# Toeplitz tiles of a second causal convolution: loaded into 32 partitions and widened twice on chip, with taps copied eight channels at a time

## The chip, the cores and the metric

The kernel runs on one core of a Trainium2 chip. The metric is the device time of one execution in microseconds (us); lower is better. The work of the five engines (TensorE, VectorE, ScalarE, GpSimd and SyncE, which only issues transfers here) is written out by hand with semaphores; nothing is scheduled by a compiler.

## The reference, cut to what matters

The input u has 16 sequences of 512 positions and 256 channels. A layer of long convolutions is followed by a feed-forward layer with a spiking activation; each is added to its input and normalised.

```python
q = u Wq + bq;  k = u Wk + bk;  v = u Wv + bv              # each [b, channel, position]
k = causal_conv(k, k_kernel) + k_D * k                     # 512 taps per channel, written with FFTs
kv = k * v
y = causal_conv(kv, ssm_kernel) + D * kv                   # 512 taps per channel
x = layernorm(u + (y * q) Wo + bo)
h = square(relu(x W_fc));  y = h W_proj
out = layernorm(x + spike_count(y) / 5)                    # five steps of a leaky integrator
```

## The kernel before, in words

**Phase 1** (to about 490 us) makes y * q. A causal convolution of one channel is a product with a Toeplitz matrix: 512 by 512, lower triangular, each diagonal holding one tap. Only one block row of it is distinct, so a channel needs a tile of 128 partitions by 512 columns in which row p is the tap sequence shifted right by p, and a mask that zeroes what lies before tap 0. Taps are split into two float16 parts, hence two such tiles a channel. The skip factors k_D and D are added to tap 0.

The 256 channels go in 32 groups of 8 (`NG`, `G`), one per step; a group's tiles are in two halves of 4 channels. In step g TensorE does three things, in this order: it projects k, v and q for a quarter of the batch and the next chunk of 32 channels (`project`, L666, 96 matmuls), it runs the first convolution of group g (`conv1`, L688, two halves of 48 matmuls) and the second convolution of group g - 1 (`conv2`, L688, as many). Four steps make a chunk. The tiles of the first convolution have two places in `T` (halves 0 to 3, used in turn), those of the second have one (halves 4 and 5), except in the last four groups, where every second group goes into `T2`. So the load of a half for the second convolution can only be issued when TensorE is done with the same half of the group before.

**Where tiles come from.** The scaled and split taps of both convolutions are written to DRAM once (`ksplit_dram`), and from there copied into 16 copies each (`kpad_dram`), with 128 zeros ahead. `spread(piece)` (L293) copies the taps of one chunk of 32 channels: for each convolution one DMA of 1 MB in packets of 4 KB, DRAM to DRAM. Eight pieces make the whole; piece 0 is copied before the first tile is loaded, 1 to 3 right after the first six tile loads, and 4 to 7 at the start of steps 0, 4, 8 and 12. `load_windows` (L305) loads one half (4 channels, two parts each, 512 columns: 8 KB a partition) into partitions 0 to 63: partition p reads from copy p // 4, starting p elements early, so that each row is shifted by one. That is 512 KB in 64 packets of 8 KB, four for each copy.

**What is done on chip with a half.** VectorE zeroes the triangle that holds no tap (`mask`, L975, 64 x 512 float16). Partitions 64 to 127 are the same rows shifted right by 64 more columns, so they are a copy of partitions 0 to 63, 3584 elements a partition: for the first convolution ScalarE makes it (`copy_windows`, L442; VectorE takes one half in the last four groups, L983), for the second VectorE does (`windows2`, L992). The first 64 columns of the upper partitions are zeroed once, ahead (`t_zero`).

**The order on each queue in step g.** SyncE: at the start of a chunk the projection weights (L311) and a spread; after each half of conv1(g), the same half of the first convolution's tiles for g + 2; after each half of conv2(g - 1), the same half of the second's for g. VectorE: `times_q(g - 2)` (L1018), the masks of the first convolution's g + 1, the two masks and the two copies of the second's g - 1, `read_projection` (L951, L954 twice), which frees TensorE's next projection, and `times_v(g)` (L1012). ScalarE: the two copies for g + 1, then two roundings to float16 (L436, L452), each followed by a subtraction on GpSimd (L571, L578) that makes the low part. All engines run their own list in order.

Three lines say how a half is loaded, where a step issues it, and in which order VectorE widens:

```python
sp.dma_start(windows[0:HP]..., bass.AP(first.tensor, first.offset, [[ROWS - HP // NCOPY, NCOPY], [-1, HP // NCOPY], [1, row]]))
sp.wait_ge(c2_half, 2 * before + half + 1); load_windows(1, half, g)
for half in range(2): mask(1, s, g, half)          # then: for half in range(2): tensor_copy(*shifted(...))
```

**Phase 2** (from about 490 us) takes the 16 sequences one by one through Wo, the first normalisation, the feed-forward layer and the second normalisation. The change does not touch it.

Of the kernel before, what the change touches and what calls it, by code (L numbers as in the profile page):

```python
# [13 lines left out]
P = 128  # L14
B, L, D, F = 16, 512, 256, 1024
# [5 lines left out]
CH = 32  # L21
NC = D // CH
G = 8
# [3 lines left out]
HP = P // 2  # L27
ROWS = P + D * 2 * L
NCOPY = 16
SLICE = CH * 2 * L  # L30
EARLY = 4
# [40 lines left out]
def build(nc, uT, u, wcat, wk_n, wv_n, bias, bo, k1, k2, kd1, kd2, woT, wfT, wpT, out):  # L72
# [11 lines left out]
    with ExitStack() as ctx:  # L84
# [3 lines left out]
        def sem(name):  # L88
            return ctx.enter_context(nc.semaphore(name))
# [112 lines left out]
        kpad_out = [sem(f"kpad_out{n}") for n in range(NC)]  # L202
# [5 lines left out]
        c1_copied_dve, c1_half, c2_half = (sem(n) for n in ("c1_copied_dve", "c1_half", "c2_half"))  # L208
# [52 lines left out]


# [15 lines left out]
        def _(sp):  # L278
# [8 lines left out]
            def spread(piece):  # L287

                at, n = piece * SLICE, SLICE // NCOPY
                for conv in range(2):  # L290
                    src = ksplit_dram[conv, at:at + SLICE].rearrange("(r n) -> r n", n=n)
                    dst = kpad_dram[conv, :, P + at:P + at + SLICE].rearrange("k (r n) -> r k n", n=n)
                    sp.dma_start(dst, src.unsqueeze(1).to_broadcast([NCOPY, NCOPY, n])).then_inc(kpad_out[piece], 16)  # L293

            def load_windows(conv, half, g):


                row = HG * 2 * L
                first = kpad_dram[conv, 0, P + (2 * g + half) * row:]
                if g % GPC == 0 and conv == 0 and half == 0:  # L300
                    sp.wait_ge(kpad_out[g // GPC], 32)
                second_place = conv == 1 and g >= NG - GPC and g % 2 == 0
                slot = 6 + half if second_place else 4 + half if conv else g % 2 * 2 + half
                windows = windows_of(conv, g % PAIR, half, g >= NG - PAIR)
                sp.dma_start(windows[0:HP].rearrange("p c a n -> p (c a n)"),  # L305
                             bass.AP(first.tensor, first.offset, [[ROWS - HP // NCOPY, NCOPY], [-1, HP // NCOPY], [1, row]])
                             ).then_inc(t_in[slot], 16)
# [13 lines left out]
            spread(0)  # L321
            sp.wait_ge(kpad_head, 16)
            sp.wait_ge(kpad_out[0], 32)
# [3 lines left out]
            for piece in range(1, EARLY):  # L327
                spread(piece)
# [11 lines left out]
            for s in range(NG):  # L340
# [4 lines left out]
                if s % GPC == 0 and s // GPC + EARLY < NC:  # L345
                    spread(s // GPC + EARLY)
# [510 lines left out]
        def _(dve):  # L857
# [16 lines left out]

            nc.vector.memset(T[HP:P].rearrange("p k c a n -> p (k c a) n")[:, :, 0:HP], 0.0).then_inc(t_zero, 1)
            link(nc.vector.memset(part_max[:, :], 0.0))
# [86 lines left out]
            def mask(conv, s, g, half):  # L963
# [10 lines left out]
                tri = windows_of(conv, s, half, final(g))[0:HP].rearrange("p c a n -> p (c a) n")[:, :, 0:HP]  # L974
                nc.vector.tensor_tensor(tri, tri, causal[0:HP, 0:HP].unsqueeze(1).to_broadcast([HP, 2 * HG, HP]),  # L975
# [9 lines left out]
            def windows2(s, g):  # L985


                for half in range(2):
                    mask(1, s, g, half)
                for half in range(2):  # L990
                    dve.wait_ge(c2_masked, 2 * g + half + 1)
                    nc.vector.tensor_copy(*shifted(windows_of(1, s, half, final(g)))).then_inc(c2_copied, 1)  # L992

            dve.wait_ge(id_done, 2)
            dve.wait_ge(t_zero, 1)
# [45 lines left out]
            for s in range(PAIR):  # L1041
                step(s, NG - PAIR, s < GPC, NC - 2)
                if s == GPC - 1:
                    nc.vector.memset(T2[HP:P].rearrange("p k c a n -> p (k c a) n")[:, :, 0:HP], 0.0
                                     ).then_inc(t_zero, 1)
                    dve.wait_ge(t_zero, 2)
# [148 lines left out]
```

## Time and profile before

| what | value |
|---|---|
| median of 3 runs | 957.03 us (953.26 to 958.75) |
| the profiled execution, its own time | 956.07 us |
| its span in the trace | 954.3 us |
| mean granted TensorE clock | 0.926 |
| TensorE busy (matmuls / weight loads) | 764.2 / 564.0 us |
| VectorE, ScalarE, GpSimd busy | 698.8, 516.9, 397.3 us |
| moved by the data queue of SyncE | 114.71 MB |

The span runs from the first to the last instruction of the trace; the device time holds 1.8 us more. Busy times overlap; what bounds the kernel is where an engine stands idle and who ends that idle time. All times in the rows below are microseconds from the span's start.

### The profile page before, as it was taken

To read this page: it belongs to the slowest core of one execution; us is meant where nothing else is said; L and a number is where in the kernel's file an instruction comes from. 1 tells how busy PE (TensorE), PEld (TensorE's weight loads), DVE (VectorE), ACT (ScalarE), POOL (GpSimd) and SP (SyncE) were. 2 spreads that over 40 slices of the span, in tenths; PEclk is the share of its full clock that TensorE was granted. 3 is DMA by queue.
4 is the path that set the end of the run, shared out by engine and by line. 5 is a ranking of instruction groups with operands and counts; after the bars stand their busy time and mean duration, and the time that the engine had idled before them with its cause. 6 is when DMAs were issued, how large, how long until landed. Compare 5 with 4: busy or idle time off the path is not lost.

```text
span 954.3 us, 26601 instructions
## 1 busy us (share of the span) xinstructions
PE 764.2 (80%) x11392; PEld 564.0 (59%) x11392; DVE 698.8 (73%) x1087; ACT 516.9 (54%) x560; POOL 397.3 (42%) x307
## 2 busy tenths in 40 slices
PE   0086877777857878776476999999999999999993
PEld 0086877777857868776464555555555555555541
DVE  6982666556464655666575689999999999999886
ACT  2474755566563665543332565665655566665662
POOL 0361222212221222221014677666666777666642
PEclk9998898899888998988776999999999999999997
DMA  9899697979885878779931001111111101111001
GB/s 341 305 277 284 149 255 172 246 169 240 178 181 118 180 159 178 175 165 197 239 90 37 8 1 45 44 44 44 44 44 44 38 10 40 44 44 45 23 22 45
DMA packets 39294, 118.37 MB, mean 124 GB/s; under 512 B 3872, under 2 KB 23200, under 8 KB 31008
## 3 DMA queue, kind: packets, MB, share of 16 engines
q1 hardware_dynamic: 37824, 114.71, 47.1%
q10 hardware_dynamic: 1376, 2.23, 0.6%
q8 instruction: 81, 1.33, 0.6%
q14 instruction: 13, 0.11, 0.0%
HBM read 106.69 MB, written 27.01 MB: 140 GB/s over the span
## 4 chain that ended last, share of the span: by engine, by line
PE 29%; DVE 22%; DMA 20%; POOL 15%; issue 12%; ACT 2%; SPq 0%; DVEq 0%; POOLq 0%; ACTq 0%
DMA arena<-kpad_dram 17%; POOL arena L612 12%; PE ps L688 11%; DVE arena L1127 7%; PE ps L666 5%; PE ps L784 5%; PE ps L791 4%; DVE arena L992 2%; DVE arena L1084 2%; DVE arena L1124 2%; PE ps L765 2%; DVE arena L1103 2%; DVE arena L975 1%; DVE arena L1109 1%; PE ps L746 1%
## 5 line engine op out<-in xcount | busy, mean ns | idle before, releaser
L688 PE MATMUL ps<-arena 128*128 128x64 f16 (+3 forms) x6144 | 190.1, 187 | 85.2 <-DVE arena L992 42.4
L688 PEld LDWEIGHTS ps<-arena 128*128 128x128 f16 x6144 | 185.2, 101 | 88.7 <-issue 87.3
L442 ACT ACTIVATE arena<-arena 64x3584 f16<-64x3584 f16 x60 | 188.6, 3182 | 54.7 <-DVE arena L975 54.7
L666 PE MATMUL ps<-arena 128*128 128x96 f16 x3072 | 147.9, 213 | 72.5 <-DVE arena L937 51.1
L666 PEld LDWEIGHTS ps<-arena 128*128 128x128 f16 x3072 | 142.3, 102 | 75.2 <-issue 68.9
L612 POOL TENSOR_TENSOR arena<-arena 128x512 f16<-128x512 f32 x128 | 178.8, 1429 | 14.6 <-ACT arena L494 14.2
L975 DVE TENSOR_TENSOR arena<-arena 64x512 f16<-64x512 f16 x128 | 65.0, 515 | 154.6 <-DMA arena<-kpad_dram 154.4
L791 PE MATMUL ps<-arena 128*128 128x512 f16 x768 | 173.2, 379 | 2.7 <-POOL arena L612 2.7
L784 PE MATMUL ps<-arena 128*128 128x512 f16 x768 | 170.8, 379 | 0.9 <-issue 0.9
L571 POOL TENSOR_TENSOR arena<-arena 128x512 f16<-128x512 f32 x32 | 42.8, 1339 | 282.3 <-ACT arena L436 282.3
L1116 DVE TENSOR_TENSOR arena<-arena 128x512 f32<-128x512 f32 x128 | 137.6, 1128 | 10.4 <-POOL arena L612 9.0
L490 ACT ACTIVATE arena<-ps,read_factor 128x512 f32<-128x512 f32 x128 | 88.0, 687 | 79.5 <-PE ps L784 62.6
L791 PEld LDWEIGHTS ps<-arena 128*128 128x128 f16 x768 | 73.9, 98 | 90.4 <-POOL arena L612 9.5
L784 PEld LDWEIGHTS ps<-arena 128*128 128x128 f16 x768 | 74.4, 98 | 86.9 <-issue 1.4
L1127 DVE SCALAR_TENSOR_TENSOR arena<-ps,stair_at,arena 128x512 bf16<-128x512 f32 x128 | 96.1, 751 | 4.5
L494 ACT ACTIVATE arena<-arena 128x512 f16<-128x512 f32 x128 | 79.3, 623 | 29.2 <-DVE arena L1116 28.0
L478 ACT ACTIVATE arena<-arena 128x256 f32<-128x256 f32 x128 | 66.3, 589 | 35.2 <-DVE arena L1095 34.7
L616 POOL TENSOR_TENSOR arena<-arena,eps 128x4 f32<-128x4 f32 x32 | 11.7, 366 | 137.1 <-DVE arena L1089 137.1
L992 DVE COPY arena<-arena 64x3584 f16<-64x3584 f16 x64 | 67.7, 1097 | 1.0
L436 ACT ACTIVATE arena<-arena 128x512 f16<-128x512 f32 x32 | 20.1, 630 | 84.0 <-DVE arena L951 83.9
L765 PE MATMUL ps<-arena 128*128 128x256 f32 x256 | 63.0, 403 | 1.2 <-ACT arena L471 1.2
L578 POOL TENSOR_TENSOR arena<-arena 128x512 f16<-128x512 f32 x32 | 38.8, 1211 | 56.0 <-ACT arena L452 56.0
(94 smaller groups left out, 707.5 us busy)
## 6 DMA issues: line engine op xcount, KB each, us to landing
arena<-kpad_dram SPq DMA_DIRECT2D x128, 512.0 KB, 6.8
kpad_dram<-ksplit_dram SPq DMA_DIRECT2D x16, 1024.0 KB, 12.3
qy<-in_uT SPq DMA_DIRECT2D x8, 1024.0 KB, 17.3
arena<-in_u SPq DMA_DIRECT2D x16, 512.0 KB, 4.3
out<-arena SPq DMA_DIRECT2D x16, 512.0 KB, 3.0
arena<-in_k SPq DMA_DIRECT2D x2, 512.0 KB, 4.6
ksplit_dram<-arena ACTq DMA_DIRECT2D x2, 512.0 KB, 3.9
arena<-in_wfT SPq DMA_DIRECT2D x1, 1024.0 KB, 12.6
```

The source lines that it names most:

```text
L442: nc.scalar.activation(*shifted(windows_of(0, s, half)), ACT.Copy).then_inc(c1_copied, 1)
L490: nc.scalar.activation(relu_h[:, f], PH[:, f % 2], ACT.Relu, scale=read_factor[:, 4:5]).then_inc(relu_ready, 1)
L494: nc.scalar.activation(h16[:, 0, f], h_square[:, f % 4], ACT.Copy).then_inc(h_hi, 1)
L612: nc.gpsimd.tensor_tensor(h16[:, 1, f], h_square[:, f % 4], h16[:, 0, f], ALU.subtract).then_inc(h_lo, 1)
L666: last = nc.tensor.matmul(o, u16[:, x, t, tok:tok + P], wcur[:, r, w, t], start=(k == 0), stop=(k == 3 * DT - 1))
L688: last = nc.tensor.matmul(out[:, ch * COL + delta * B:(ch + 1) * COL], win[:, delta * P:(delta + 1) * P], data(xp, ch)[:, 0:cols], start=( ...
L765: last = nc.tensor.matmul(PW[:, j // 2, (j % 2) * D:(j % 2 + 1) * D], yT[:, t, j * P:(j + 1) * P], wo[:, t], start=(t == 0), stop=(t == DT ...
L784: last = nc.tensor.matmul(PH[:, f % 2], wf16[:, w, t, f * P:(f + 1) * P], x16[:, r, x, t], start=(k == 0), stop=(k == 3 * DT - 1))
L791: return nc.tensor.matmul(PD[:, t], wp16[:, w, f, t * P:(t + 1) * P], h16[:, h, f], start=first, stop=last)
L992: nc.vector.tensor_copy(*shifted(windows_of(1, s, half, final(g)))).then_inc(c2_copied, 1)
L1116: nc.vector.tensor_tensor(h_square[:, f % 4], relu_h[:, f], relu_h[:, f], ALU.mult).then_inc(square_ready, 1)
L1127: ins = nc.vector.scalar_tensor_tensor(c, y, stair_at[:, n:n + 1], c, ALU.is_gt, ALU.add)
```

## The change

The second convolution's half is loaded into partitions 0 to 31 only (32 packets of 8 KB, 256 KB, two from each copy). VectorE masks 32 x 256 elements, then copies partitions 0 to 31 to 32 to 63, shifted by 32 columns (`shifted_quarter`, 3840 elements a partition), for both halves, then 0 to 63 to 64 to 127 as before. The first 32 columns of partitions 32 to 63 are zeroed once, in `T` and in `T2`. The first convolution's tiles are loaded as before.

The taps are spread by group, eight channels at a time: each DMA writes 256 KB in packets of 1 KB (16 x 16 x 512 elements). Groups 0 to 2 are copied before the first tile load, 3 to 7 after the first six tile loads, and each step s copies group s + 8. Each group's first tile load waits for its own copy.

```diff
-SLICE = CH * 2 * L
-EARLY = 4
+SLICE = G * 2 * L
+AHEAD = 8
+NKP = 2 * AHEAD
...
+        def shifted_quarter(windows):
+            t = windows.rearrange("p c a n -> p (c a) n")
+            return t[QP:HP, :, QP:L], t[0:QP, :, 0:L - QP]
...
-                at, n = piece * SLICE, SLICE // NCOPY
+                at, n = g * SLICE, SLICE // 16
...
-                    sp.dma_start(dst, src.unsqueeze(1).to_broadcast([NCOPY, NCOPY, n])).then_inc(kpad_out[piece], 16)
+                    sp.dma_start(dst, src.unsqueeze(1).to_broadcast([16, NCOPY, n])).then_inc(kpad_out[g % NKP], 16)
...
-                if g % GPC == 0 and conv == 0 and half == 0:
-                    sp.wait_ge(kpad_out[g // GPC], 32)
+                if conv == 0 and half == 0:
+                    sp.wait_ge(kpad_out[g % NKP], 32 * (g // NKP + 1))
...
-                sp.dma_start(windows[0:HP].rearrange("p c a n -> p (c a n)"),
-                             bass.AP(first.tensor, first.offset, [[ROWS - HP // NCOPY, NCOPY], [-1, HP // NCOPY], [1, row]])
+                parts = QP if conv else HP
+                sp.dma_start(windows[0:parts].rearrange("p c a n -> p (c a n)"),
+                             bass.AP(first.tensor, first.offset,
+                                     [[ROWS - parts // NCOPY, NCOPY], [-1, parts // NCOPY], [1, row]])
...
-            spread(0)
+            for g in range(3):
+                spread(g)
             sp.wait_ge(kpad_head, 16)
-            sp.wait_ge(kpad_out[0], 32)
...
-            for piece in range(1, EARLY):
-                spread(piece)
+            for g in range(3, AHEAD):
+                spread(g)
...
-                if s % GPC == 0 and s // GPC + EARLY < NC:
-                    spread(s // GPC + EARLY)
+                if s + AHEAD < NG:
+                    spread(s + AHEAD)
...
+            nc.vector.memset(T[QP:HP, 4:6].rearrange("p k c a n -> p (k c a) n")[:, :, 0:QP], 0.0).then_inc(t_zero, 1)
...
-                tri = windows_of(conv, s, half, final(g))[0:HP].rearrange("p c a n -> p (c a) n")[:, :, 0:HP]
-                nc.vector.tensor_tensor(tri, tri, causal[0:HP, 0:HP].unsqueeze(1).to_broadcast([HP, 2 * HG, HP]),
+                n = QP if conv else HP
+                tri = windows_of(conv, s, half, final(g))[0:n].rearrange("p c a n -> p (c a) n")[:, :, 0:n]
+                nc.vector.tensor_tensor(tri, tri, causal[0:n, 0:n].unsqueeze(1).to_broadcast([n, 2 * HG, n]),
...
                 for half in range(2):
                     dve.wait_ge(c2_masked, 2 * g + half + 1)
+                    nc.vector.tensor_copy(*shifted_quarter(windows_of(1, s, half, final(g)))).then_inc(c2_widened, 1)
+                for half in range(2):
+                    dve.wait_ge(c2_widened, 2 * g + half + 1)
                     nc.vector.tensor_copy(*shifted(windows_of(1, s, half, final(g)))).then_inc(c2_copied, 1)
```

SyncE's list at the start, before the change. `kpad_dram<-ksplit_dram` is a spread, `arena<-kpad_dram` a load of tiles, `arena<-w_dram` the projection weights:

```order
L293 DMA kpad_dram<-ksplit_dram 16x16x2048 [waits ksplit_out]
L293 DMA kpad_dram<-ksplit_dram 16x16x2048
L305 DMA arena<-kpad_dram 64x1x4096 [waits kpad_out0,kpad_head]
L305 DMA arena<-kpad_dram 64x1x4096 x5
L293 DMA kpad_dram<-ksplit_dram 16x16x2048 x6
L311 DMA arena<-w_dram 128x384 [waits proj]
L293 DMA kpad_dram<-ksplit_dram 16x16x2048 x2
L305 DMA arena<-kpad_dram 64x1x4096 [waits c1_half] x4
L305 DMA arena<-kpad_dram 64x1x4096 [waits c2_half] x2
```

And as changed, from the same place (its line numbers are those of the changed file):

```order
L302 DMA kpad_dram<-ksplit_dram 16x16x512 [waits ksplit_out]
L302 DMA kpad_dram<-ksplit_dram 16x16x512 x5
L315 DMA arena<-kpad_dram 64x1x4096 [waits kpad_out0,kpad_head]
L315 DMA arena<-kpad_dram 64x1x4096
L315 DMA arena<-kpad_dram 64x1x4096 [waits kpad_out1]
L315 DMA arena<-kpad_dram 64x1x4096
L315 DMA arena<-kpad_dram 32x1x4096 x2
L302 DMA kpad_dram<-ksplit_dram 16x16x512 x10
L322 DMA arena<-w_dram 128x384 [waits proj]
L302 DMA kpad_dram<-ksplit_dram 16x16x512 x2
L315 DMA arena<-kpad_dram 64x1x4096 [waits kpad_out2,c1_half]
L315 DMA arena<-kpad_dram 64x1x4096 [waits c1_half]
```

Ahead of the first tile load stand 1.5 MB of copies where 2 MB stood, and between the first six loads and the loads for group 2 stand 3 MB where 8 MB stood. In the steps after that a spread of 0.5 MB stands in each step, right behind the second convolution's loads and ahead of the first's:

```order
L302 DMA kpad_dram<-ksplit_dram 16x16x512 x2
L315 DMA arena<-kpad_dram 64x1x4096 [waits kpad_out4,c1_half]
L315 DMA arena<-kpad_dram 64x1x4096 [waits c1_half]
L315 DMA arena<-kpad_dram 32x1x4096 [waits c2_half] x2
L302 DMA kpad_dram<-ksplit_dram 16x16x512 x2
```

VectorE's list in one step before the change, from `times_q` (L1018) to `times_v` (L1012); `t_in` are the landings of halves, `c2_masked` is the mask's own end:

```order
L1018 SCALAR_TENSOR_TENSOR qy<-ps,read_factor,qy 128x512 [waits c2_half]
L975 TENSOR_TENSOR arena<-arena 64x8x64 [waits t_in2]
L975 TENSOR_TENSOR arena<-arena 64x8x64 [waits t_in3]
L975 TENSOR_TENSOR arena<-arena 64x8x64 [waits t_in4]
L975 TENSOR_TENSOR arena<-arena 64x8x64 [waits t_in5]
L992 COPY arena<-arena 64x8x448 [waits c2_masked] x2
L951 SCALAR_TENSOR_TENSOR arena<-ps,read_factor,arena 128x512 [waits k_lo,proj]
```

And as changed:

```order
L1034 SCALAR_TENSOR_TENSOR qy<-ps,read_factor,qy 128x512 [waits c2_half]
L988 TENSOR_TENSOR arena<-arena 64x8x64 [waits t_in2]
L988 TENSOR_TENSOR arena<-arena 64x8x64 [waits t_in3]
L988 TENSOR_TENSOR arena<-arena 32x8x32 [waits t_in4]
L988 TENSOR_TENSOR arena<-arena 32x8x32 [waits t_in5]
L1005 COPY arena<-arena 32x8x480 [waits c2_masked] x2
L1008 COPY arena<-arena 64x8x448 [waits c2_widened] x2
L963 SCALAR_TENSOR_TENSOR arena<-ps,read_factor,arena 128x512 [waits k_lo,proj]
```

Two copies of both halves now stand between the second half's mask and the copy that TensorE waits for, where none stood; the lists of TensorE, ScalarE and GpSimd hold the same instructions in the same order as before.

## Rows read from the trace of the kernel before

**Rows 1.** The page: busy us, share, instructions; in 40 slices, clock and DMA share in tenths
```profile
PE 764.2 (80%) x11392; PEld 564.0 (59%) x11392; DVE 698.8 (73%) x1087; ACT 516.9 (54%) x560; POOL 397.3 (42%) x307
...
PEclk9998898899888998988776999999999999999997
DMA  9899697979885878779931001111111101111001
```

**Rows 2.** Busy time by stretch: PE, PEld, DVE, ACT, POOL (instructions), clock, DMA share, GB/s
```profile
14.00:30.00 16.00, 0.00 (x0) 0.00 (x0) 14.80 (x18) 7.03 (x6) 5.88 (x4) 1.00 1.03 412
50.00:62.00 12.00, 8.37 (x177) 8.22 (x176) 10.69 (x9) 11.89 (x8) 7.79 (x2) 0.99 1.00 216
66.00:81.00 15.00, 13.19 (x341) 12.84 (x338) 9.19 (x13) 7.64 (x5) 6.07 (x4) 1.00 1.03 332
438.00:475.00 37.00, 19.02 (x539) 18.52 (x539) 21.83 (x30) 12.08 (x7) 4.83 (x5) 0.72 1.02 230
97.00:437.00 340.00, 265.83 (x7575) 261.04 (x7576) 194.60 (x292) 196.21 (x105) 64.91 (x53) 0.90 0.80 183
```

**Rows 3.** Chain that ended last, 97 to 437 us: shares by line
```profile
by line: DMA arena<-kpad_dram 35.7%; PE ps L688 27.1%; issue 13.7%; PE ps L666 12.2%; DVE arena L992 5.0%; DVE arena L975 2.1%; ACT arena L442 1.9%; DVE arena L951 0.9%; DVE qy L954 0.5%; DVE arena L954 0.5%; POOL arena L571 0.4%; ACT arena
```

**Rows 4.** The same chain piece by piece, 325 to 385 us: start, us, what
```profile
325.10 5.73 DMA arena<-kpad_dram
330.85 0.43 DVE arena L975
331.30 1.10 DVE arena L992
332.54 2.66 PE ps L688 x96
335.22 8.05 DMA arena<-kpad_dram
...
374.95 9.47 DMA arena<-kpad_dram
```

**Rows 5.** Who waited for whom on PE, 97 to 438 us: us in total, times, longest
```profile
PE ps L688 <- DVE arena L992: 30.5, 14, 7.2
PE ps L688 <- issue: 29.7, 15, 4.6
PE ps L666 <- issue: 16.6, 10, 7.4
```

**Rows 6.** The page, DMA queues: packets, MB, share of 16 engines
```profile
q8 instruction: 81, 1.33, 0.6%
```

**Rows 7.** Timeline around one wait of PE inside a projection
```profile
335.43 2.00 PE L666 MATMUL ps<-arena 128*128 128x96 f16 x43 [0.24 <-DVE qy L954]
339.78 2.43 PE L666 MATMUL ps<-arena 128*128 128x96 f16 x53 [2.35 <-issue]
```

**Rows 8.** The chain piece by piece, 36 to 101 us
```profile
37.27 8.52 DMA kpad_dram<-ksplit_dram
46.48 6.91 DMA arena<-kpad_dram
53.41 3.57 DVE arena L975
...
78.20 17.33 DMA arena<-kpad_dram
```

**Rows 9.** Timeline of the start: GpSimd's split beside the mask, PE's third projection, first wait of step 1
```profile
52.60 4.11 POOL L584 TENSOR_TENSOR arena<-qy,arena 128x2048 f16<-128x2048 f32 x1 [14.41 <-ACT arena L430]
61.15 5.86 PE L666 MATMUL ps<-arena 128*128 128x96 f16 x96 [3.63 <-DVE arena L937]
97.91 3.67 PE L688 MATMUL ps<-arena 128*128 128x64 f16 x96 [7.17 <-DVE arena L992]
```

**Rows 10.** Groups by shape on VectorE, 97 to 438 us: busy, mean ns | idle before
```profile
L992 DVE COPY arena<-arena 64x3584 f16<-64x3584 f16 x54 | 56.4, 1084 | 0.8
L975 DVE TENSOR_TENSOR arena<-arena 64x512 f16<-64x512 f16 x104 | 51.2, 497 | 127.9 <-DMA arena<-kpad_dram 127.7
```

**Rows 11.** The chain piece by piece, 437 to 490 us
```profile
441.17 15.03 DMA arena<-kpad_dram
...
478.33 4.97 DMA arena<-kpad_dram
```

More of the change, by code:

```diff
@@ L27 @@
 HP = P // 2
+QP = P // 4
 ROWS = P + D * 2 * L
 NCOPY = 16
-SLICE = CH * 2 * L
-EARLY = 4
+SLICE = G * 2 * L
+AHEAD = 8
+NKP = 2 * AHEAD
 NU = 8
@@ L201, in build @@
             sem(n) for n in ("kpad_zero", "kpad_hi", "kpad_lo", "kpad_head", "ksplit_out", "w16_out"))
-        kpad_out = [sem(f"kpad_out{n}") for n in range(NC)]
+        kpad_out = [sem(f"kpad_out{n}") for n in range(NKP)]
         t_in = [sem(f"t_in{n}") for n in range(8)]
@@ L207, in build @@
             sem(n) for n in ("t_zero", "c1_masked", "c2_masked", "c1_copied", "c2_copied"))
-        c1_copied_dve, c1_half, c2_half = (sem(n) for n in ("c1_copied_dve", "c1_half", "c2_half"))
+        c1_copied_dve, c1_half, c2_half, c2_widened = (
+            sem(n) for n in ("c1_copied_dve", "c1_half", "c2_half", "c2_widened"))
         ld_wcur = [sem(f"ld_wcur{r}") for r in range(2)]
@@ L286, in _, with spread @@
                              uT.rearrange("(t p) n -> p t n", p=P)[:, :, n * UP:(n + 1) * UP]).then_inc(ld_u[n], 16)
-            def spread(piece):
-                at, n = piece * SLICE, SLICE // NCOPY
+            def spread(g):
+                at, n = g * SLICE, SLICE // 16
                 for conv in range(2):
@@ L991, in windows2 @@
                     dve.wait_ge(c2_masked, 2 * g + half + 1)
+                    nc.vector.tensor_copy(*shifted_quarter(windows_of(1, s, half, final(g)))).then_inc(c2_widened, 1)
+                for half in range(2):
+                    dve.wait_ge(c2_widened, 2 * g + half + 1)
                     nc.vector.tensor_copy(*shifted(windows_of(1, s, half, final(g)))).then_inc(c2_copied, 1)
             dve.wait_ge(id_done, 2)
-            dve.wait_ge(t_zero, 1)
+            dve.wait_ge(t_zero, 2)
             for quarter in range(GPC):
@@ L1045, in _ @@
                                      ).then_inc(t_zero, 1)
-                    dve.wait_ge(t_zero, 2)
+                    nc.vector.memset(T2[QP:HP].rearrange("p k c a n -> p (k c a) n")[:, :, 0:QP], 0.0
+                                     ).then_inc(t_zero, 1)
+                    dve.wait_ge(t_zero, 4)
                 if s == PAIR - 2:
```

## The prediction

> **What bounds the kernel now.** I looked first at the page's busy times and slices [rows 1]: the DMA engines are busy in the first 21 slices of 24 us and nearly idle after, so the change, which touches loads and copies of tiles, acts on phase 1 alone, the first 490 us. The table by stretch [rows 2] then gives the rates. Tile loads alone (50 to 62 us) run at 216 GB/s with the DMA engines fully busy, loads into 128 partitions (14 to 30 us) at 412, the DRAM copies (66 to 81 us) at 332. Over 97 to 437 us, 26 steps of 13.1 us each, the DMA share is 0.80 and the clock 0.90: no resource is full. So it is a loop of waits. The chain's shares [rows 3] name it: tile loads 35.7%, both convolutions 27.1%, unnamed "issue" 13.7%, the projection 12.2%, VectorE's copy 5.0%.
>
> The pieces [rows 4] show the loop of the second convolution, whose tiles have one place: conv2 ends, its second half's load is issued and lands 5.7 us later where nothing is ahead of it and 8.1 to 9.5 where the first convolution's loads are; then one mask (0.43), one copy (1.10), TensorE (2.66 for both halves), and the next load. Beside it TensorE has its own path of projection and conv1, and waits twice over [rows 5]: 30.5 us on VectorE's copy, and 46.3 us in 25 waits for nothing that is named, 1.8 us a step. One such wait, 2.35 us, stands in the middle of a projection [rows 7], after 43 of 96 matmuls, where the code has no semaphore. The instruction queue moves 1.33 MB in 81 packets [rows 6], 16 KB each, on the same DMA engines. I take the unnamed waits to be late instructions.
>
> **Part 1, the loop of the second convolution.** Removed: half the bytes. A half is 256 KB, so both halves are 0.5 MB less; at 216 GB/s [rows 2] that is 2.4 us. With other loads ahead all of it shortens the landing of the second half. With nothing ahead, a 512 KB load takes 4.97 us [rows 11]: 2.4 of data and 2.6 that stay. A half then lands after 3.8 us, and the second, issued some 1.6 us after the first, after about 3.8 where it took 5.7 [rows 4]: 1.9 less. Added behind the last landing: two copies of 3840 elements. The copy of 3584 takes 1.084 us [rows 10], so each takes about 1.17, together 2.34; the copy that TensorE waits for comes after both. The mask has half the elements (256 for 512 a partition) and falls from 0.43 to about 0.25. Net: 2.34 - 0.18 - 2.4 = -0.24 us behind other loads, 2.34 - 0.18 - 1.9 = +0.26 with none. Both cases occur, the first more often: -0.1 a step, -3 us over 26 steps. The bounds: 2.7 us gained (0.5 MB at the 183 GB/s of the whole stretch, [rows 2]) gives -0.5 a step, 1.2 us gained (its own bytes only) gives +0.95.
>
> **Part 2, VectorE's list.** It gains 2.34 - 0.36 = 2.0 us a step on 7.5 (194.6 us in 26 steps, [rows 2]). It stood idle 127.7 us for tiles [rows 10], 4.9 a step, so the work fits in front of nothing new: 9.5 of 13.1 us. What is queued behind the copies is `read_projection`, for which the next projection waits; it follows the last copy by the same distance as before. GpSimd's subtractions come after it and so miss the added copies. ScalarE's copies of the first convolution's tiles depend on loads that are not later. I cost all this at nothing; its cover is that idle time, and without it each step would pay up to 2.0.
>
> **Part 3, the late instructions.** An instruction packet takes its turn on a DMA engine behind packets of 8 KB. A step had 256 of these and has 192, a quarter fewer. A quarter of 1.8 us is 0.45 a step, 12 us in all; where TensorE comes sooner, the loop of part 1 is late next, so I take half, -6 us. Bounds: 0 and -26 (1.0 a step).
>
> The trace has TensorE stop after 43 matmuls with no semaphore there, and 46.3 us of such waits [rows 5, 7]. The Trainium skill, page "Runtime: NRT & Kernel Launch", section "Instruction fetch mechanics", says that instructions come in blocks of 16 KiB and that crossing a block is mostly hidden. The block's size agrees with the 81 packets for 1.33 MB; "mostly hidden" does not agree with the 2.35 us, unless that wait has another cause. By that rule part 3 would be nothing and the sum 939.
>
> **Part 4, the spreads.** The same 16 MB are copied, in packets of 1 KB where they were 4 KB. No row has a DRAM copy in such packets. The near bound is the rate of the 4 KB copies, 332 GB/s: 0.5 MB take 1.6 us. The far one is four times the packets at the same time each, 6.3 us a step. I take 1.6 to 2, near the row, since bytes and not packets fill the engines in every stretch of rows 2. In a step they stand behind the second convolution's loads, when the engines have some 2 us of idle (0.20 of 13.1 us), so the first convolution's loads pay under 1 us, and these are needed a step later: nothing. SyncE issues two more DMAs a step, 0.6 us each, while it waits anyway.
>
> **Part 5, the start.** The chain [rows 8]: spread 8.52 us, tile load 6.91, a mask of 3.57, and later a load of 17.33. (a) Ahead of the first tiles go 1.5 MB instead of 2, and the wait covers only the first 0.5. At 332 GB/s the tiles land about 4 us sooner, near 49.5. VectorE is busy until 51.7, so the mask then starts before GpSimd's 4.11 us split [rows 9], beside which it took 3.57 us. The third projection at 61.15 comes 3 us sooner; it is held then by GpSimd's split, which ends at 56.7. (b) The 17.33 us load stood behind 8 MB of spreads; now 3 MB, of which 2.5 are through (7.9 us) before it is issued. It takes about 7.5. Issued 3 us sooner, it lands near 83 instead of 95.5; masks, widening and copy add 4, and conv2(0) starts at 87 instead of 97.9 [rows 9]. Part 5: -11 us. Bounds: -4 if the small packets take twice as long, -14.
>
> **Part 6, the last four steps.** From 438 to 475 us the DMA share is 1.02 at 230 GB/s [rows 2]: here the engines are the bound, and one load takes 15.03 us [rows 11]. Four groups of the second convolution save 2 MB, 9 us; the added copies come back on the path in two of four steps (5 us). -4; bounds +3 and -9. Two more memsets: 0.4 us, at the start beside loads and once in this part.
>
> **Sum.** -3 - 6 - 11 - 4 = -24 us. The profiled execution took 956.07, which gives 932; it lies 1 us under the median of the runs, so 933.
>
> **The rivals.** *A, the widening costs more than the load gives back* (slower). The place is the loop of part 1: if the fixed part of a landing decides and only the half's own bytes count, the landing shrinks by 1.2 us against 2.16 added, +0.95 a step. Over 30 steps +28; part 5 keeps -11: 956 + 28 - 11 + 1 = 974. It decides from a landing less than 2.16 us shorter. For it: the 5.73 and 4.97 us landings, half of which is not data. Against it: the 8.05 and 9.47 us ones. The Trainium skill, page "SBUF — State Buffer", section "The DMA setup-cost knee", has a transfer pay about 2 µs whatever its size, which is on this side; rows 11 have it at 2.6. Chance 0.15.
> *B, packets of 1 KB are slow.* 4 us a step for the spread: engines 7.1 + 4 = 11.1 of 13 us, loads land later by 0.5 in the 24 steps that copy, +12, the start gains 4, the end 4, parts 1 and 3 nothing: 956 + 12 - 8 + 1 = 961. Chance 0.12.
> *C, the unnamed waits have nothing to do with DMA traffic.* They stay as they are, and part 3 falls out of the sum. The stop in the middle of the projection speaks for instructions being late, not for traffic as the reason: 939. Chance 0.12.
> *D, instructions are the real bound.* TensorE's 22784 instructions [rows 1] came in 81 packets, 281 in each, and a step has 576: two packets a step, and if one takes 6 us to come, that is the step. Relieved, part 3 gives 26 us and part 1 its best, 14, of which 7 overlap: 956 - 33 - 11 + 1 = 913. Chance 0.13.
> *E, only part of the start is gained* (6 us) and all else is covered: 951. Chance 0.08.
> My forecast, 920 to 937, has 0.40.
>
> **How the numbers follow.** The likeliest case gives 933. A measurement of this kernel can tell about 0.5% (4.8 us) from no change. Faster by more: the forecast, C, D and half of E, 0.69. Within: E's other half, part of B, 0.11. Slower: A and half of B, 0.20. The range leaves out A and a little below D: 911 to 962.
>
> **What would show it.** The chain's loads in the loop near 3.8 to 6 us, followed by a 0.25 us mask, 2.3 us of new copies and 1.1 us; the steps at 12.8 us; conv2(0) at 87 us; GB/s near 155 in the steps. If landings stay above 6 us, A or B; the new spreads' share tells which. If unnamed waits of PE stay at 1.8 us a step, C; under 1, D. I am wrong if conv2(0) does not start before 93 us, or if VectorE's copies, and not loads, lead PE's waits by more than 60 us.

## The result and the profile after

| | before | changed |
|---|---|---|
| median | 956.38 us (4 runs) | 926.86 us (4 runs, 923.85 to 931.76) |
| ratio, 95% interval | | 0.9698 (0.9647 to 0.9749) |
| span of the profiled execution | 954.3 us | 922.0 us |
| conv2(0) starts | 97.9 | 86.9 |
| one step, from there to the end of conv1(27), 26 steps | 12.95 | 12.17 |
| from there to the last conv2 | 53.7 | 54.7 |
| the rest (phase 2) | 465.8 | 463.9 |

The lower rows are worked out from the starts and ends of the matmuls in the two traces. Of 32.3 us, 11.0 came at the start, 20.4 in the steps and 1.9 in phase 2, which the change does not touch (463.8 to 466.7 in all kernels below); the last steps gave back 1.0. The page of the changed kernel, granted clock and DMA share in 40 slices:

```profile
PEclk9999899998988898987669999999999999999997
DMA  9976777777756776668400011100111110011001
```

The mean clock of the span is as before, 0.926 (1 is TensorE's level of 2.4 GHz, 0.5 that of 1.2 GHz; the figure of a stretch is the mean over both). The DMA share is lower in most slices of phase 1 after the first two. Its table by stretch (PE, PEld, DVE, ACT, POOL, then clock, DMA share, GB/s), whose first row answers to that of 97 to 437 us in [rows 2], then the steps and the last steps:

```profile
97.00:437.00 340.00, 274.77 (x7779) 270.09 (x7776) 260.37 (x364) 198.11 (x107) 67.18 (x54) 0.87 0.73 172
...
86.90:403.40 316.50, 265.11 (x7488) 260.72 (x7488) 240.80 (x336) 193.49 (x104) 65.13 (x52) 0.89 0.71 168
403.40:458.00 54.60, 33.28 (x961) 32.88 (x960) 48.56 (x61) 13.35 (x9) 7.75 (x6) 0.69 0.67 170
```

The same for the kernel before, its steps and its last steps:

```profile
97.90:434.70 336.80, 263.53 (x7488) 258.71 (x7488) 191.44 (x288) 194.68 (x104) 64.85 (x52) 0.90 0.80 183
434.70:488.40 53.70, 31.77 (x962) 31.10 (x961) 34.69 (x45) 13.34 (x9) 7.20 (x6) 0.75 0.93 217
```

TensorE issues the same 7488 matmuls in 20 us less. They kept it busy for 10.1 us a step before and 10.2 now; its idle time fell from 2.8 to 2.0 us a step. So the gain of the steps is waiting and not clock. In the last steps the DMA share fell from 0.93 to 0.67, and VectorE's busy time rose from 34.7 to 48.6 of some 54 us. The chain of the last steps, before and then changed, shows that the bound moved from transfers to VectorE:

```profile
by line: DMA arena<-kpad_dram 37.2%; PE ps L688 25.1%; issue 15.7%; DVE arena L992 9.5%; DVE part_max L884 4.3%; DVE arena L975 3.0%; POOL arena L571 2.4%; DVE arena L983 2.0%; DVE arena L951 1.4%; ACT arena L436 1.2%
```

```profile
by line: DVE arena L1005 26.2%; PE ps L699 20.2%; DVE arena L1008 14.0%; DVE part_max L896 8.2%; DMA arena<-kpad_dram 8.2%; DVE arena L988 6.6%; issue 5.4%; DVE qy L1034 4.1%; DVE arena L996 4.0%; DVE arena L1028 2.7%; DVE part_max L1072 0.
```

The clock fell there too, from 0.75 to 0.69, and the same matmuls took 33.3 us where they took 31.8; the last steps' +1.0 us has this in it. The chain of the changed kernel, piece by piece, 324 to 385 us:

```profile
347.76 6.76 DMA arena<-kpad_dram
...
354.55 0.29 DVE arena L988
...
354.86 2.23 DVE arena L1005 x2
...
357.11 1.10 DVE arena L1008
...
358.34 3.83 PE ps L699 x96
...
362.19 3.85 DMA arena<-kpad_dram
```

It answers to [rows 4]: the mask is 0.29 us instead of 0.43, the two widenings (2.23) are new, and the load is 3.85 us with nothing ahead of it, 6.76 behind others, instead of 5.73 and 8.05. The other groups of VectorE, 98 to 400 us, answer to [rows 10]:

```profile
L1005 DVE COPY arena<-arena 32x3840 f16<-32x3840 f16 x48 | 53.2, 1146 | 0.8
L1008 DVE COPY arena<-arena 64x3584 f16<-64x3584 f16 x50 | 52.2, 1084 | 0.8
L988 DVE TENSOR_TENSOR arena<-arena 64x512 f16<-64x512 f16 x49 | 31.7, 660 | 32.0 <-DMA arena<-kpad_dram 32.0
L988 DVE TENSOR_TENSOR arena<-arena 32x256 f16<-32x256 f16 x48 | 13.4, 278 | 29.3 <-DMA arena<-kpad_dram 29.2
```

And who PE waited for in that stretch, before and then changed:

```profile
PE ps L688 <- DVE arena L992: 28.0, 13, 7.2
PE ps L688 <- issue: 26.0, 12, 4.6
PE ps L666 <- issue: 16.1, 9, 7.4
```

```profile
PE ps L699 <- DVE arena L1008: 30.9, 19, 4.1
PE ps L677 <- issue: 8.8, 5, 7.3
PE ps L699 <- issue: 8.7, 7, 2.6
```

The wait for tiles stayed where it was (28.0 and 30.9 us). The unnamed waits fell from 42.1 to 17.5 us. That is where the steps' gain shows.

### The profile page after: what moved, and what is told of

Same layout as the page of the kernel before. It is cut to its first block, busy times and chain, and to the rows that moved or that the text cites. A ratio compares the mean times of both kernels' runs of the same rounds, so it can differ in the third digit from the quotient of the medians.

```text
span 922.0 us, 26738 instructions
## 1 busy us (share of the span) xinstructions
PE 761.8 (83%) x11392; PEld 563.3 (61%) x11392; DVE 761.9 (83%) x1153; ACT 517.1 (56%) x560; POOL 397.5 (43%) x307
## 3 DMA queue, kind: packets, MB, share of 16 engines
q10 hardware_dynamic: 1376, 2.23, 0.7%
## 4 chain that ended last, share of the span: by engine, by line
DVE 33%; PE 28%; POOL 15%; DMA 14%; issue 8%; ACT 1%; POOLq 0%; DVEq 0%; ACTq 0%
DMA arena<-kpad_dram 13%; POOL arena L623 13%; PE ps L699 11%; DVE arena L1145 7%; DVE arena L1005 6%; PE ps L795 5%; PE ps L677 5%; PE ps L802 4%; DVE arena L1008 3%; DVE u_maxima L896 2%; DVE arena L1102 2%; DVE arena L1142 2%; PE ps L776 2%; DVE arena L1121 2%; DVE arena L1127 1%
## 5 line engine op out<-in xcount | busy, mean ns | idle before, releaser
L623 POOL TENSOR_TENSOR arena<-arena 128x512 f16<-128x512 f32 x128 | 178.8, 1428 | 14.7 <-ACT arena L505 14.2
L582 POOL TENSOR_TENSOR arena<-arena 128x512 f16<-128x512 f32 x32 | 42.7, 1337 | 256.2 <-ACT arena L447 256.2
L988 DVE TENSOR_TENSOR arena<-arena 64x512 f16<-64x512 f16 (+1 forms) x128 | 56.5, 459 | 73.1 <-DMA arena<-kpad_dram 72.8
L1005 DVE COPY arena<-arena 32x3840 f16<-32x3840 f16 x64 | 71.9, 1161 | 1.0
L776 PE MATMUL ps<-arena 128*128 128x256 f32 x256 | 61.0, 394 | 1.2 <-ACT arena L482 1.2
```

What stands on the lines that cost most here:

```text
L623: nc.gpsimd.tensor_tensor(h16[:, 1, f], h_square[:, f % 4], h16[:, 0, f], ALU.subtract).then_inc(h_lo, 1)
L776: last = nc.tensor.matmul(PW[:, j // 2, (j % 2) * D:(j % 2 + 1) * D], yT[:, t, j * P:(j + 1) * P], wo[:, t], start=(t == 0), stop=(t == DT ...
L1005: nc.vector.tensor_copy(*shifted_quarter(windows_of(1, s, half, final(g)))).then_inc(c2_widened, 1)
```

## The experiments

All ran with the kernel before on the same chip; ratios are to it. The kernel before has one trace, the one read ahead of the prediction; on the chips of the experiments its median was 958.28 to 962.08 us, so a difference of a few us between its trace and theirs can be the chip's. "Busy (clock)" is what TensorE's matmuls took in a step, and the granted clock over the steps. "Unnamed" is PE's wait on "issue" in 98 to 400 us, "tiles" its wait for VectorE's copy there. Two executions of the changed kernel differ in them by 8.6 and 5.2 us (17.5 and 26.1; 30.9 and 25.7), so less than that says nothing.

| kernel | ratio (95% interval) | conv2(0) | step | busy (clock) | last steps | unnamed | tiles |
|---|---|---|---|---|---|---|---|
| before | 1 | 97.9 | 12.95 | 10.14 (0.90) | 53.7 | 42.1 | 28.0 |
| changed | 0.9698 (0.9647 to 0.9749) | 86.9 | 12.17 | 10.20 (0.89) | 54.7 | 17.5 | 30.9 |
| changed, again (e10) | 0.9707 (0.9664 to 0.9749) | 87.7 | 12.30 | 10.15 (0.90) | 52.7 | 26.1 | 25.7 |
| e1 spreads alone | 0.9784 (0.9728 to 0.984) | 85.8 | 12.79 | 10.37 (0.87) | 55.5 | 37.1 | 21.5 |
| e2 widening alone | 0.981 (0.9751 to 0.9869) | 97.9 | 12.71 | 10.33 (0.88) | 53.9 | 27.3 | 31.7 |
| e4 e1 and the widening copies | 1.015 (1.009 to 1.0209) | 87.6 | 13.90 | 10.90 (0.81) | 59.8 | 23.0 | 44.7 |
| e3 by halves | 0.9666 (0.9593 to 0.9739) | 86.5 | 12.31 | 10.17 (0.92) | 52.4 | 32.1 | 14.1 |
| e5 changed, first widening cut short | 0.9475 (0.9432 to 0.9518) | 85.8 | 11.71 | 9.98 (0.92) | 46.2 | 32.0 | 10.7 |
| e7 changed, 1 MB more a step | 0.9875 (0.9829 to 0.992) | 87.8 | 12.93 | 10.35 (0.89) | 52.1 | 38.0 | 23.4 |
| e8 changed, packets of 4 KB | 0.9646 (0.9603 to 0.9689) | 87.3 | 12.26 | 10.13 (0.91) | 53.0 | 16.8 | 33.8 |
| e9 e3, end copies on ScalarE | 0.9638 (0.9591 to 0.9685) | 85.7 | 12.37 | 10.35 (0.90) | 52.0 | 28.3 | 17.5 |
| e11 changed, PE loop written out | 0.9635 (0.9588 to 0.9681) | 87.3 | 12.16 | 10.14 (0.90) | 53.0 | 25.6 | 22.9 |
| e12 e9 and e11 | 0.9611 (0.9572 to 0.9649) | 86.4 | 12.12 | 10.21 (0.90) | 52.1 | 26.5 | 15.8 |
| e13 changed, no spreads in the steps | 0.9693 (0.9649 to 0.9737) | 87.1 | 12.48 | 10.24 (0.89) | 53.5 | 25.5 | 26.2 |

**Which half of the change does what.** e1 undoes the widening, e2 undoes the spreads:

```diff
-                parts = QP if conv else HP                                       # e1
+                parts = HP
...
-                    nc.vector.tensor_copy(*shifted_quarter(windows_of(1, s, half, final(g)))).then_inc(c2_widened, 1)
...
-SLICE = G * 2 * L                                                                # e2
-AHEAD = 8
+SLICE = CH * 2 * L
+EARLY = 4
...
-                if s + AHEAD < NG:
-                    spread(s + AHEAD)
+                if s % GPC == 0 and s // GPC + EARLY < NC:
+                    spread(s // GPC + EARLY)
```

> The changed kernel with the second convolution's tiles loaded into 64 partitions and widened once, as before: only the spreads by group are new. Theory 1 (the start comes from the spreads, the steps' gain from the smaller loads): conv2(0) starts near 87 us instead of 97.9, the steps stay near 12.95 us, the time is 11 to 14 us under before, 943 to 946. Theory 2 (the steps' gain comes from spreading evenly and in small packets, the widening pays for its own load): steps near 12.3 us, time 928 to 934.

> The changed kernel with the taps copied as before, 32 channels at a time in packets of 4 KB: only the 32-partition loads and the two widenings are new. Theory 1: conv2(0) near 97 to 99 us, steps near 12.2 us, last stretch no shorter, 936 to 942. Theory 2: steps near 12.9 us and the added copies on top, 953 to 958.

e2 lies between the theories: nothing at the start, as theory 1 had it, and 18 us (1.9%) in all by its ratio, but steps of 12.71 us where theory 1 had 12.2 and theory 2 had 12.9, and 945.1 us, outside both. e1 gave 21 us (2.2%), more than theory 1 had and less than theory 2: the start comes early by 12.1 us, as expected, and the steps give some more. The whole of the start is thus the spreads'. Both alone come to 4.1%, together they give 3.0%, so part of what each gives in the steps is the same time, given once; the intervals (about 0.5% each) leave open how much.

**The price of the copies.** e4 adds the widening copies to e1 and gives nothing back in the load; e5 cuts the first widening of the changed kernel to 32 of its 480 columns:

> The spreads by group and the 64-partition loads and masks of before, and the widening copies on top (they write what the load brought already): the price of the two added copies with nothing given back by the load. If the copies stand on the loop that sets the steps: 2.3 us a step over the spread-only kernel, times 30, 60 us, so 1000 to 1010. Rival: TensorE waits for instructions and other things often enough that half is covered, 970 to 985. If VectorE's idle time covers them, 943 to 950.

> The changed kernel with the first widening cut to 32 of its 480 columns, so partitions 32 to 63 of the second convolution's tiles hold mostly zeros (this part of the computation is left out): what the two added copies still cost. If the loop through load, mask, two widenings and copy sets the steps, 2.2 us a step go, 26 steps and the last four: 865 to 875. If the steps follow TensorE's supply of instructions instead (by the sum of its unnamed stalls and its waits for tiles, which was 50 us for the changed kernel and 50 us again with the order by halves), what is not waited for tiles is waited for instructions: steps 11.8 to 12.1, the last stretch 6 to 8 us shorter because VectorE is its bound, 908 to 918.

```diff
-            return t[QP:HP, :, QP:L], t[0:QP, :, 0:L - QP]     # e5
+            return t[QP:HP, :, QP:QP + 32], t[0:QP, :, 0:32]
```

From e1 to e4 the step grows by 1.11 us and the last steps by 4.3: 35 us (3.7%), half of the price of 2.3 us a step. From the changed kernel to e5 the step shrinks by 0.46 and the last steps by 8.5 us. So in a step the two copies cost 0.5 to 1.1 us, not 2.3.

Not all of that is waiting. The steps of e1 and then of e4, by stretch:

```profile
85.80:418.40 332.60, 269.69 (x7495) 265.38 (x7496) 189.36 (x288) 195.48 (x104) 65.12 (x52) 0.87 0.86 202
```

```profile
87.60:449.20 361.60, 283.48 (x7488) 279.80 (x7488) 258.61 (x338) 192.70 (x103) 64.11 (x52) 0.81 0.79 185
```

The same matmuls took 13.8 us longer in e4, at a granted clock of 0.81 instead of 0.87. That is 0.53 of the 1.11 us a step; 0.58 are idle time. The order holds in every run (over the whole span 0.916 to 0.929 in e1, 0.888 to 0.904 in e4), and the other way in e5 (0.937 to 0.950 against 0.921 to 0.934 in the changed kernel), where the matmuls account for 0.2 of the 0.46 us a step and 3.5 of the 8.5 us at the end. In e5 half the partitions of the second convolution's tiles also hold mostly zeros, and the runs do not part what moved the clock. Both first expectations fell; the rival that half is covered held, and so did "11.8 to 12.1, the last stretch 6 to 8 us shorter" nearly. What covers part of the copies can be read from e5's waits of PE, 98 to 400 us:

```profile
PE ps L677 <- issue: 16.3, 9, 6.2
PE ps L699 <- issue: 15.7, 12, 2.1
PE ps L699 <- DVE arena L1008: 10.7, 11, 2.1
```

The wait for tiles fell by 20 us against the changed kernel, the unnamed one rose by 15 (by 15 and 6 against its second trace). e3 shows the same: 14.1 us for tiles, 32.1 unnamed. From e4 to the changed kernel only the second convolution's load is halved, and its mask with it: the step falls by 1.73 us, 45 us in 26 steps (1.03 of it idle time, 0.70 shorter matmuls). That is the worth of the smaller load, against 1.11 for the copies.

**Is it late instructions, and what makes them late?** Timing first. In the kernel before, a packet of the instruction queue starts within 336.9 to 337.0 us:

```profile
q8 instruction: 1, 0.02, 84.6%
```

The wait of [rows 7] ends at 339.78, 1.4 us after this packet's 16 KB have come. All packets can be gone through like this. Between 95 and 405 us the fourteen traces have 247 breaks of over 0.3 us inside a block of matmuls, where the code has no semaphore. Every one of them ends 1.07 to 1.81 us after an instruction packet has landed, and those that belong to successive packets lie 126 to 128 matmuls apart. So these waits are late instruction packets; this is shown, and not only argued from one wait.

Then the jump. The twelve traces of kernels with the loop have a stop of 4.2 to 7.4 us between steps 15 and 16, where TensorE's loop over eight steps jumps back. In the changed kernel it is this row of PE's timeline:

```profile
263.31 6.18 PE L677 MATMUL ps<-arena 128*128 128x96 f16 x96 [7.28 <-issue]
```

```diff
-            with pe.Fori(1, NC // 2 - 1) as pair:
+            for pair in range(1, NC // 2 - 1):          # e11
```

> The changed kernel with TensorE's loop over steps 8 to 23 (two passes of eight steps) written out, so that its instruction stream has no jump back; all else as it was. In every trace so far TensorE stands still for 6 to 7.5 us between step 15 and step 16, where that jump is. If late instructions are the cause of its unnamed stops, this one goes: 4 to 7 us less, 920 to 923. If the stop is another engine's (all of them jump back there), nothing changes.

> The changed kernel itself, on the same chip as the next three: 0.965 to 0.975 of the kernel before.

The stop is gone; the same place in e11's timeline:

```profile
252.69 5.19 PE L699 MATMUL ps<-arena 128*128 128x64 f16 x192
258.21 2.03 PE L677 MATMUL ps<-arena 128*128 128x96 f16 x44 [0.33 <-DVE qy L966]
260.45 2.38 PE L677 MATMUL ps<-arena 128*128 128x96 f16 x52 [0.21 <-issue]
```

The work and every semaphore are the same, VectorE's and ScalarE's loops still jump there, and 7 us of waiting went away: this stop was TensorE's own instruction stream. By the ratios (0.9635 against 0.9707) about 7 us reached the end, but their intervals overlap a little. Then traffic, in both directions:

> The changed kernel with 1 MB more of traffic in each of steps 2 to 27: a DRAM to DRAM copy in 128 packets of 8 KB, right behind the second convolution's loads, to a place that nobody reads. Its packets take as long on the engines as the saved half of those loads did. If DMA traffic delays TensorE's instructions, the stalls inside matmul blocks (12 us from conv2(0) to the end of conv1(27) in the changed kernel, 39 before) rise to 25 us or more and the steps from 12.2 to 12.7 at least, 940 to 948. If those stalls have another cause they stay near 12 us, and the time rises by less than 6 us, 926 to 933.

> The changed kernel without the copies of taps in the steps: tiles of group g are loaded from the taps of group g mod 8 (the rest of the taps is left out of the computation). It takes 1 MB of DRAM traffic (0.5 MB written) out of steps 1 to 23. If traffic delays TensorE's instructions, stalls inside blocks fall from 12 us to under 8 and the steps by 0.2 to 0.5, 913 to 922; what is freed may show as waits for tiles instead, since VectorE's copies are next in line. If traffic has no part, 924 to 929.

> The changed kernel with each tile load as two DMAs of two channels, so that its packets are 4 KB instead of 8 KB: same bytes, same places. If instructions wait their turn behind long packets, stalls inside blocks fall under 8 us and the time by 3 to 10 us, 917 to 924. If it is the bytes and not the packet's length, stalls stay at 12 us and the time within 4 us of the changed kernel, or rises by up to 10 through 8 more DMAs a step on SyncE.

```diff
+                if 1 < s < NG - GPC:                                             # e7, behind conv2's loads
+                    sp.dma_start(dummy_dram[s], dummy_src).then_inc(dummy_sem, 16)
...
-                if s + AHEAD < NG:                                               # e13
-                    spread(s + AHEAD)
...
-                first = kpad_dram[conv, 0, P + (2 * g + half) * row:]
+                first = kpad_dram[conv, 0, P + (2 * (g % AHEAD) + half) * row:]
...
+                for x in range(2):                                               # e8
+                    cs = slice(x * HG // 2, (x + 1) * HG // 2)
...
+                                         [[ROWS - parts // NCOPY, NCOPY], [-1, parts // NCOPY], [1, row // 2]])
```

The "stalls inside blocks" of these expectations are breaks of over 0.15 us between the starts of two matmuls of one block of 48 or 96: 39.1 us before, 12.4 in the changed kernel's first trace, 22.7 in its second. e7 has 37.6 of them, a step of 12.93 us, 16 us more in all: as expected if traffic delays instructions. e13 takes traffic away and gains nothing: stalls of 22.5, a share of 0.60 where e7 has 0.90 (e7 and then e13):

```profile
98.00:400.00 302.00, 238.64 (x6658) 233.96 (x6655) 215.45 (x302) 175.28 (x93) 56.56 (x46) 0.89 0.90 242
```

```profile
98.00:400.00 302.00, 245.71 (x6890) 241.76 (x6891) 221.74 (x312) 179.96 (x97) 59.52 (x48) 0.89 0.60 129
```

The stalls alone do not prove it: e3, e5, e9, e11 and e12 have 28 to 32 us of them at shares of 0.73 to 0.77, without more traffic, where TensorE waits less for tiles. The packets tell more. On average the next instruction packet starts 2.6 us after TensorE has entered a block in the kernel before, e1 and e7 (shares of 0.80, 0.88 and 0.90), 1.6 and 1.9 us in the two traces of the changed kernel (0.72 and 0.73), 2.1 in e4 (0.81) and 1.8 to 2.3 in all others. These are means over 34 to 55 blocks of a trace, placed by counting matmuls from stop to stop, and single ones range from nothing to over 5 us. So near full engines do delay the packets, by 0.7 to 1.0 us each against the changed kernel; at 0.77 and less the delay does not follow the share (1.8 in e13 at 0.60, 2.3 in e3 at 0.74). Halving the packets' length (e8) changed nothing that can be measured either (0.9646 against 0.9698 and 0.9707, unnamed waits 16.8): its second expectation, "it is the bytes". e7 has a weakness: its copy also stands ahead of the next tile loads, and the runs do not say how many of its 16 us are that and how many the later packets, though the wait for tiles (23.4) is no longer than in the changed kernel.

**Versions that might be faster.** e3 finishes one half before the other; e9 adds that ScalarE makes both copies of the first convolution's tiles in the last four steps; e12 adds e11:

```diff
                 for half in range(2):                                            # e3
                     mask(1, s, g, half)
-                for half in range(2):
                     dve.wait_ge(c2_masked, 2 * g + half + 1)
                     nc.vector.tensor_copy(*shifted_quarter(...)).then_inc(c2_widened, 1)
-                for half in range(2):
                     dve.wait_ge(c2_widened, 2 * g + half + 1)
```

> The changed kernel, with VectorE finishing the first half (mask, widen, copy) before it takes up the second. If the loop of the second convolution sets the steps, the first half is ready at least 1.2 us sooner after the last landing and the second half about 0.3: steps 0.5 to 1.2 us shorter, 26 steps and the last four, 895 to 912. Rival: the steps now follow TensorE's own path (projection, conv1, late instructions), then less than 5 us are gained, 922 to 926. Second rival: the second half comes too late for TensorE, no gain or up to 5 us slower.

> The order by halves, and in the last four steps ScalarE makes both copies of the first convolution's tiles instead of leaving one to VectorE. VectorE was busy 0.89 of the last stretch (55 us), so 1.09 us less for it in each of four steps: 3 to 5 us off the last stretch, 920 to 925. Rival: ScalarE's two copies in a row (6.4 us) come too late for conv1 there, and nothing is gained.

> The order by halves, both copies of the first convolution's tiles on ScalarE in the last four steps, and TensorE's loop written out: the best version I have. The first two gave 0 to 5 us against the changed kernel, the third should give 4 to 7: 915 to 922. If supply of instructions sets the pace, the order by halves adds nothing and the time is that of the unrolled kernel within 3 us.

e3 alone: no gain that can be told (929.24 us beside 962.08 of the kernel before; 0.9666 and 0.9698 overlap), although its first expectation had 15 us and more. The unnamed waits stand at 32.1 us where the changed kernel has 17.5 and 26.1: its first rival. e9's last steps took 52.0 us, e3's 52.4: its rival too. e12 is faster than the changed kernel on the same chip, 920.85 against 929.35 us, with intervals apart (0.9572 to 0.9649 and 0.9664 to 0.9749). It beats both kernels, by 1.0 and 3.9%. How much of the 1.0 is e11's (0.7 by its own ratio, with intervals that overlap) is not settled.

## Why the prediction was right, and where it was mis-sized

It said 933 us in 911 to 962, faster; 926.86 came out. By its parts, in the trace:

- **Part 5, the start: -11 forecast, -11.0 measured.** conv2(0) at 87 us, as said. The chain's 17.33 us load [rows 8] became this piece (forecast 7.5):

```profile
75.98 6.62 DMA arena<-kpad_dram
```

  The mask started before GpSimd's split; in the timeline:

```profile
51.81 0.74 DVE L988 TENSOR_TENSOR arena<-arena 64x512 f16<-64x512 f16 x2
52.53 1.99 ACT L443 ACTIVATE arena<-qy,d_scale 128x2048 f16<-128x2048 f32 x1
52.72 4.10 POOL L595 TENSOR_TENSOR arena<-qy,arena 128x2048 f16<-128x2048 f32 x1 [14.41 <-ACT arena L441]
```

  Two masks took 0.74 us where one had taken 3.57. The third projection came 2.1 us sooner (59.02), not 3.

- **Part 4, the spreads: nothing forecast, nothing found.** e13, which takes them out of the steps, gains nothing, and e1 with them is 2.2% faster than the kernel before; rival B is out.
- **Parts 1 and 3, the steps: -9 forecast, -20.4 and -17 in two executions.** The direction and the mechanism held, the size did not. The step that failed is part 1's balance, "2.34 - 0.18 - 2.4 = -0.24 us", which set the whole 2.34 against the landing. As single times its terms were good: 3.85 us for a load with nothing ahead (3.8 forecast), 1.146 a widening (1.17), 0.28 the mask (0.25). But the step does not follow this loop alone. TensorE waits for tiles in some steps and for instructions in others, so the copies cost 1.11 us a step (e4 against e1), half of it as longer matmuls at a lower clock, which the sum did not have, and the smaller load brought 1.73 (changed against e4), partly by another way than the landing: -0.6 a step, 16 us, where I had -0.1, 3 us. Part 3 looked at the right rows (the unnamed waits fell by 16 to 25 us, I had taken half of 12) and named the right cause, late instruction packets. They start 0.7 to 1.0 us sooner after TensorE enters a block than in the kernel before, over a quarter of the 2.6 us; taking a quarter of the waits, and then half of that for the overlap, was too little. But the count of packets of 8 KB is not a rule for it: neither their length (e8) nor fewer bytes below a share of 0.73 (e13) counts.
- **Part 6, the last steps: -4 forecast, +1.0 and -1.0 measured.** "5 us come back" was too little: 8.5 us do (e5: 46.2 against 54.7 us), because VectorE is the bound there once transfers are not; 3.5 of the 8.5 us are matmuls at a higher clock, 0.82 where it was 0.69.
- **Part 2, VectorE's list, "at nothing":** right in the steps (TensorE waited for `read_projection` 9 times, 2.2 us in all, where it was 1.2 before), wrong in the last four. It also had GpSimd's subtractions miss VectorE's added work; the copies do, but the first convolution's masks now meet them (last section).

Rival A is out by e4 and the changed kernel (1.73 against 1.11), rival E by the 11.0 us of the start. Rival D, instructions as the real bound, is half true: unnamed waits take up part of whatever time is freed (e3, e5), but they did not hold the step at its length, which fell to 11.71 us in e5. By the sign set for it, unnamed waits under 1 us a step, it was met in one trace of the changed kernel and not in the other (0.7 and 1.1), and its 913 us did not come. Its packets of 281 instructions are 252 to 256 by the distance of the stops. Rival C is out: the unnamed waits fell, and the packets come later where the engines are near full.

Of the other signs the mask (0.29), the copies (2.23 and 1.10) and the loads (3.85 to 6.76) came nearly as said; the steps gave 12.17 us for 12.8, and 168 GB/s for 155. That the total of 927 lies so near 933 is partly luck: 11 to 8 us too little in the steps were met by 5 to 3 too much in the last ones. One sum of its chances is off by a hundredth: slower, A and half of B, is 0.21 and not 0.20.

The Trainium skill, page "Runtime: NRT & Kernel Launch", section "Instruction fetch mechanics", also says that a taken branch to a target outside the two blocks at hand forces a fetch of the target before execution goes on: the 7.28 us stop that e11 removed agrees. Its "mostly hidden" for plain block crossings does not: e12, without that jump, still waits 26.5 us in 302 for nothing that is named, and its breaks inside blocks end on instruction packets as in all traces.

**What stays open.** Why traffic counts at a share of 0.8 to 0.9 and not at 0.6 to 0.7, how e7's delay divides between instructions and tiles, and what lowers the clock when the copies are added (e4). No kernel here changed the number of TensorE's instructions alone; that was not tried.

## What to carry to other kernels

Two waits that take turns on one engine hide each other: price a change by running one side alone and both together, since here 2.3 us of copies on the apparent loop cost 1.1, and 20 us less waiting for tiles (e5) came back as 15 us of other waiting. Look at the granted clock of the same stretch as well: half of that 1.1 us was not waiting but slower matmuls. An "issue" wait in the middle of a block without semaphores is worth a look at the instruction queue: if it ends just after a packet there, it is late instructions. A loop with few passes over a long body may be cheaper written out (7 us for one jump here). When transfers stop being the bound of a stretch, look at once at what is busy 60% and more beside them: in the last steps VectorE took over, and the saving was gone.

## What the runs showed of the hardware

- Packets of 1 KB, DRAM to DRAM, cost little: one took 51 ns on average in the changed kernel's steps, one of 4 KB 171 ns in those of the kernel before. 64 DMAs of 256 KB landed in 5.2 us at the median against 12.3 for 16 of 1 MB, and without them in the steps (e13) the kernel was no faster.
- TensorE's instructions come in packets of 16 KB, each good for 126 to 128 matmuls with their weight loads. Where it had to wait for one, it went on 1.07 to 1.81 us after the landing, and two such stops on successive packets were never less than 3.7 us apart (123 pairs in 14 traces, median 5.8). 128 matmuls of a convolution take an estimated 3.5 us at full clock (96 took 2.65), so a convolution can outrun its instructions even where nothing delays them.
- A 64 x 512 mask on VectorE takes 0.41 to 0.42 us alone and up to 1.38 when it runs beside one of GpSimd's subtractions. In the changed kernel's timeline three masks, 64 x 512 twice and 32 x 256 (0.28 us) once, took 1.73 us where 1.11 was due:

```profile
314.56 1.16 POOL L589 TENSOR_TENSOR arena<-arena 128x512 f16<-128x512 f32 x1 [0.58 <-ACT arena L463]
314.80 1.73 DVE L988 TENSOR_TENSOR arena<-arena 64x512 f16<-64x512 f16 x3
```

  In the changed kernel more masks fall into such a moment, 31 of 49 in 98 to 400 us against 23 of 92 before, and their mean rises from 498 to 660 ns (26 of 48 and 613 ns in its second trace); before, one mask at the start took 3.57 us beside GpSimd's 4.11. The Trainium skill, page "SBUF — State Buffer", section "Who interferes with whom", has a VectorE instruction with two SBUF inputs contend with a GpSimd instruction that reads SBUF; these durations agree.
- A load of 256 KB into 32 partitions landed in 3.85 us with nothing ahead, one of 512 KB into 64 in 4.97.
